# Moving the first edge layer's bias and maximum from ScalarE to VectorE in a graph layer, with longer lists of separately fetched rows

## The chip, the cores and the metric

The kernel runs on one core of a Trainium2 chip. The metric is the device time of one execution in microseconds (us); for the kernel before it is the median of three runs. The profile and the trace come from one execution under the hardware profiler. A core has five engines that work side by side and wait for each other through semaphores: TensorE (PE in the profile; PEld is its weight load), VectorE (DVE), ScalarE (ACT), GpSimd (POOL) and SyncE (SP). SPq and ACTq in a row are the queues of an engine that issue transfers.

## The reference

A graph of 6250 nodes with 128 numbers each has 106250 edges, sorted by their target node. For every edge a small network on its attributes is scaled by a gate, joined with the row of the source node, and sent through a second network; the results are added up by target node, and a residual and a normalisation follow. All is float32.

```python
ef = relu(edge_attr @ We1 + be1) @ We2 + be2
tw = sigmoid(timestamps[:, None] @ Wt + bt)
ef = ef * tw
combined = concatenate([x[row], ef], axis=1)
msg = relu(combined @ Wn1 + bn1) @ Wn2 + bn2
out = segment_sum(msg, col, num_segments=N) + x
x = layernorm(x + out)
```

## The kernel before

The kernel first multiplies x by the upper half of Wn1, adds bn1 and stores the result in HBM as `node_table`. The product with Wn2 is taken only after the sum over the edges, on whole nodes.

The edges are cut into 104 pairs of 1024 edges (two groups of four tiles of 128). A pair p is worked on over several steps; in step s, TensorE does these things in this order:

- psT: transposes of the edge attributes of pair s (L914), which ScalarE copies to `eaT`
- psS: sums of pair s - 3 by one-hot matrices (L896), after ScalarE's maximum on `h` (L656)
- psM: product of the edge features `efw` of pair s - 2 with the lower half of Wn1 (L938)
- psH: first layer of pair s (L951). Ahead of it stands a wait until the first six gathers of pair s - 2 have landed (`follow_gathers`)
- psE: second layer of pair s - 1 (L963), which reads `h1`

ScalarE makes `h1` from psH (`relu_h1`, L729: bias and maximum with 0 in one ACTIVATE) at the end of its step. VectorE does, in step s: two adds of found sums to `acc` (L1184), eight one-hots (L1226) and their count (L1234); then `pre` of pair s - 2 (L1220: psM plus the gathered rows, into `h`); then `second_layer` of pair s - 1 (L1241). Every two steps or so a block of 512 nodes is finished by all engines (`finish`).

The rows of `node_table` that `pre` adds are fetched by GpSimd with indirect transfers (L566), one for each tile of 128 edges, eight for a pair. The rows land in a ring of slots, four pairs deep (two spare pairs come in once, at pairs 8 and 9). Before the gathers of pair p, GpSimd waits until `pre` of enough pairs is done:

```python
def added_for(p):

    if p >= CLOSE_FROM:
        return p - 1
```

Below `CLOSE_FROM` the count is p - 3 (two less up to pair 13), which stands for `pre` of pair p - 4; from `CLOSE_FROM` on it stands for `pre` of pair p - 2.

For some pairs GpSimd leaves out the eighth gather. Its 128 rows are fetched one by one instead, by plain transfers that SyncE issues (pairs in `FETCHED`, 16 rows in a step, eight steps for a pair) or ScalarE issues (pairs in `ACT_FETCHED`, 8 rows in a step, 16 steps for a pair). They land in a buffer, and in step p + 1 ScalarE copies them to their place (`place_rows`). There are 11 pairs in the first list and 6 in the second. The first four pairs (0 to 3) come from x with 32 gathers of their own. So GpSimd issues 32 + 100 x 8 - 17 = 815 gathers.

All engines but GpSimd run the same order of steps, written out for the case that applies here (`most < W`).

Of the kernel before, what the change touches and what calls it, by code (L numbers as in the profile page):

```python
# [34 lines left out]
ALU = mybir.AluOpType  # L35
# [10 lines left out]
P = 128  # L46
# [30 lines left out]
PART = (6, PAIR * TILES - 6)  # L77


CLOSE_FROM = 20  # L80


SPARE = range(8, 10)


FETCH_ROWS, FETCH_STEPS = 16, 8
FETCHED = list(range(15, 96, FETCH_STEPS))


ACT_ROWS, ACT_STEPS, ACT_FROM = 8, 16, 6  # L90
ACT_FETCHED = list(range(ACT_FROM + ACT_STEPS, 103, ACT_STEPS))


def gnn_kernel(nc, x, src, dst, edge_attr, edge_weight, We1, be1, We2, be2, Wt, bt, Wn1, bn1, Wn2, bn2, out):
# [5 lines left out]
    PAIRS = G // PAIR  # L100
    BODY = 4
# [21 lines left out]
    with ExitStack() as ctx:  # L123
# [332 lines left out]
        def _(sp):  # L456
# [83 lines left out]
            for n in range(BODY, PAIRS):  # L540
                sp.wait_ge(eaT_ps, n - BODY + 1)
                load_edges(n)
                if n == BODY:
                    sp.wait_ge(src_in, 48)
                fetch_rows(n)
                sp.wait_ge(tw_ready, n - BODY + 1)
                load_weights_of(n)
            sp.wait_ge(last.y_done, 1)
            sp.dma_start(out_last, x_sb[0:LAST, FULL, 0:C]).then_inc(y_out, 16)

# [42 lines left out]
        def _(act):  # L593
# [44 lines left out]

            def fetch_rows(s):

                f, at = divmod(s - ACT_FROM, ACT_STEPS)
                if not 0 <= f < len(ACT_FETCHED) or at * ACT_ROWS >= P:
                    return
                if f == 0 and at == 0:
                    act.wait_ge(src_in, 48)
                    wait_table(act)
                if at == 0 and f > 1:
                    act.wait_ge(act_placed, f - 1)
                parts = range(at * ACT_ROWS, min((at + 1) * ACT_ROWS, P))
                rows = numbers_of(ACT_ENGINE, ACT_FETCHED[f], parts)  # L650
                for part, row in zip(parts, rows):
                    act.dma_start(act_fetched[part:part + 1, f % 2, :], table[bass.ds(row, 1), :])\  # L652
                        .then_inc(act_rows_in[f % 2], 16)
# [17 lines left out]
            def step(i, k):  # L671
                s = i * BODY + k
                if s >= PAIRS + 2:
                    if s == PAIRS + 2:
                        last_step((PAIRS - 1) % BODY * PAIR)
                    return
                if live(i, k, ADD_LAG):
                    copy_sums(s - ADD_LAG, k - ADD_LAG)
                if TILE < k <= TILE + BT // 2 and 1 <= i < TURNS:
                    finish_one(act, blocks, low["now"], lambda b: copy_tiles((k - TILE - 1) * 2), False)  # L680
                if live(i, k, H_LAG):
                    g = s - H_LAG
                    at = g % BODY * PAIR
                    act.wait_ge(pre_ready, g + 1)
                    relu(h[:, at:at + PAIR, :].rearrange("p q e -> p (q e)")).then_inc(h_ready, 1)
                if s - 1 in FETCHED + ACT_FETCHED:
                    place_rows(s - 1)
                if live(i, k, 0):
                    act.wait_ge(eaT_ps, s + 1)
                    nc.scalar.activation(eaT[:, k % 2, :], psT[:, :], ACT.Copy).then_inc(eaT_ready, 1)  # L690
                if s < RAW - RAW_BEFORE - 1:
                    copy_raw(s)
                if s == 0:
                    act.wait_ge(table_out[0], 16 * RING)
                    relu_h1(s)
                if s == 1:
                    act.wait_ge(table_out[1], 16 * RING)
                if live(i, k, 0):
                    if s < BODY:
                        for n in ([], [0], [1], [2, 3])[s]:  # L700
                            weigh(n)
                    else:
                        weigh(s)
                        fetch_rows(s)
                    if s:
                        relu_h1(s)
                if s == RAW - RAW_BEFORE - 2:
                    copy_raw(s + 1)
# [89 lines left out]
        def _(pe):  # L798
# [100 lines left out]
            def step(i, k):  # L899
# [45 lines left out]
                if live(i, k, 0):  # L945
                    follow_gathers(s, 0)
                    pe.wait_ge(eaT_ready, s + 1)
                    if raw and k == 0:
                        pe.wait_ge(src_e_ready, 2)
                    for a in range(2):  # L950
                        mm = nc.tensor.matmul(psH[:, a, :], we1[a * F:(a + 1) * F, :],  # L951
                                              eaT[a * F:(a + 1) * F, k % 2, :], start=True, stop=True)
                    mm.then_inc(h1_ps, 1)
                if raw and k in (0, 2):
                    raw_product(k)
                if live(i, k, EF_LAG):
                    if raw and k == EF_LAG:
                        pe.wait_ge(table_ready, len(JOBS))
                        pe.wait_ge(h1_ready, 1)
                    if isinstance(i, int) and s - EF_LAG == PAIRS - 1:  # L960
                        pe.wait_ge(h1_ready, PAIRS)
                    for r in range(2):
                        mm = nc.tensor.matmul(psE[:, r, :], we2[:, :], h1[:, (k - EF_LAG) % 2, r * GE:(r + 1) * GE],  # L963
                                              start=True, stop=True)
                    mm.then_inc(ef_ps, 1)
# [105 lines left out]
        def _(dve):  # L1071
# [167 lines left out]
            def second_layer(g, k):  # L1239
# [3 lines left out]
                                               tw[:, (k - EF_LAG) % 2, :], ALU.add, ALU.mult)\  # L1243
                    .then_inc(efw_ready, 1)

            def pre(g, i, k):
                place = (k - MSG_LAG) % BODY
                at = slice(place * PAIR, (place + 1) * PAIR)
                dve.wait_ge(msg_ps, g + 1)
                if isinstance(g, int) and g < RAW // PAIR:  # L1250
                    rows = raw_pairs[g]
                    if g < RAW_BEFORE // PAIR:
                        dve.wait_ge(table_ready, len(BLOCKS) + (g + 1) * PAIR)
                    else:
                        dve.wait_ge(raw_ready, (g + 1) * PAIR - RAW_BEFORE)
                else:
                    slot = (place - len(SPARE)) % BODY * PAIR
                    rows = rows_of(g) if isinstance(g, int) else gathered[:, slot:slot + PAIR, :]
                    for part in range(2):
                        landed, count = (landing(g, part) if isinstance(g, int)  # L1260
                                         else (gather_in[slot // PAIR][part], (i - 1) * (16 * PART[part])))
                        dve.wait_ge(landed, count)
                make_pre(h[:, at, :], psM[:, :, :], rows).then_inc(pre_ready, 1)

            def step(i, k):
# [38 lines left out]
                if isinstance(i, int) and s == 0:  # L1304
                    for r in range(2):
                        dve.wait_ge(dst_ps, 1 + r)
                        spread(dst_e, 1, r, dst_e_ready)
                    add_raw_bias(0)
                if live(i, k, MSG_LAG):
                    pre(s - MSG_LAG, i, k)  # L1310
                if isinstance(i, int) and s == 2:
# [262 lines left out]
```

## Time and profile before

| what | value |
|---|---|
| median of three runs (lowest, highest) | 1044.24 us (1042.26, 1045.14) |
| profiled execution: its own time, its span | 1044.55 us, 1043.1 us |
| busy share: TensorE, VectorE, ScalarE, GpSimd | 82%, 62%, 47%, 74% |
| mean granted clock of TensorE | 0.956 of full speed |

The span runs from the first to the last instruction. An engine's busy share counts the time in which an instruction ran; issuing transfers, waiting and reading registers are not counted as busy. In a row of the trace, "[0.39 <-PE psM L938]" says that the engine was idle for 0.39 us before, and that psM of TensorE ended that wait; "<-issue" means that it waited for nothing that the profile shows.

### The profile page before, as it was taken

What the parts mean: (1) busy time and instruction counts of PE and PEld (TensorE: products, weight loads), DVE (VectorE), ACT (ScalarE), POOL (GpSimd) and SP (SyncE); (2) the same over time, 40 slices, a digit from 0 to 9 for tenths busy, and PEclk for the clock granted to TensorE, in tenths of its full rate; (3) what the DMA queues carried; (4) which work ended last, traced back from release to release, by engine and by line L of the source; (5) the groups of instructions that cost most, each with busy time, mean ns of one, the idle gap of its engine ahead of it and who ended that gap; (6) DMA issues with size and microseconds to landing.
All of it is one profiled execution on the core that took longest, in us unless ns stands there. A gap on an engine that the chain in (4) does not pass through costs nothing.

```text
span 1043.1 us, 22424 instructions
## 1 busy us (share of the span) xinstructions
PE 851.1 (82%) x5035; PEld 616.5 (59%) x5036; DVE 648.9 (62%) x1682; ACT 494.9 (47%) x674; POOL 776.5 (74%) x825
## 2 busy tenths in 40 slices
PE   6989996988888778778787778878877877888884
PEld 6766665665556565555565555555555555565653
DVE  4767774775756665755557566566566566557566
ACT  5565454455445345444345445445444444444443
POOL 7777777777777777777777777777777777777772
PEclk9999999999999999999999999999999999999997
DMA  8984555555555554554545555455455455455311
GB/s 231 278 239 124 146 146 146 140 150 140 135 156 142 144 155 118 145 154 133 137 138 137 137 143 155 117 146 154 115 147 146 126 146 143 127 149 142 83 53 48
DMA packets 159417, 148.90 MB, mean 143 GB/s; under 512 B 123479, under 2 KB 127894, under 8 KB 159270
## 3 DMA queue, kind: packets, MB, share of 16 engines
q1 hardware_dynamic: 129062, 89.99, 31.0%
q0 software_dynamic: 26080, 53.46, 20.0%
q10 hardware_dynamic: 4128, 3.87, 1.2%
q8 instruction: 45, 0.74, 0.3%
q14 instruction: 102, 0.84, 0.3%
HBM read 140.85 MB, written 6.40 MB: 141 GB/s over the span
## 4 chain that ended last, share of the span: by engine, by line
POOL 44%; issue 22%; PE 12%; DMA 7%; DVE 6%; SPq 3%; ACT 3%; ACTq 1%; DVEq 1%; POOLq 0%
POOL gathered L566 44%; DMA gathered<-node_table,src_e 5%; PE psS L896 4%; PE psM L938 3%; PE psE L963 2%; DVE h L1220 2%; PE psH L951 2%; SPq L537 2%; DMA x_sb<-in_x 1%; DVE onehot L1226 1%; ACT h L656 1%; DMA ew<-in_edge_weight 1%; ACT tw L724 1%; ACTq L652 1%; DVE efw L1241 1%
## 5 line engine op out<-in xcount | busy, mean ns | idle before, releaser
L566 POOL DMA_INDIRECT gathered<-node_table,src_e x767 | 729.3, 951 | 234.0 <-issue 228.2
L729 ACT ACTIVATE h<-psH,be_c 128x1024 f32<-128x1024 f32 x104 | 115.9, 1114 | 443.1 <-PE psH L951 435.1
L896 PE MATMUL psS<-onehot,h 128*128 128x128 f32 x1656 | 226.4, 292 | 67.6 <-ACT h L656 65.7
L896 PEld LDWEIGHTS psS<-onehot,h 128*128 128x128 f32 x1656 | 209.1, 204 | 86.1 <-issue 49.4
L1220 DVE TENSOR_TENSOR h<-psM,gathered 128x1024 f32<-128x1024 f32 (+1 forms) x102 | 120.2, 1180 | 220.8 <-DMA gathered<-node_table,src_e 173.4
L963 PE MATMUL psE<-h,we 128*128 128x512 f32 x416 | 218.3, 649 | 0.0
L938 PE MATMUL psM<-wn,efw 128*128 128x128 f32 x1664 | 208.6, 280 | 4.8 <-DVE h L1220 4.8
L938 PEld LDWEIGHTS psM<-wn,efw 128*128 128x128 f32 x1664 | 200.7, 197 | 5.6 <-DVE h L1220 5.6
L1241 DVE SCALAR_TENSOR_TENSOR efw<-psE,be_c,tw 128x1024 f32<-128x1024 f32 x104 | 133.3, 1281 | 105.6 <-PE psE L963 95.5
L951 PE MATMUL psH<-eaT,we 64*128 64x512 f32 x416 | 120.1, 654 | 66.7 <-DMA gathered<-node_table,src_e 63.3
L1226 DVE TENSOR_SCALAR onehot<-split_ids,dst_e 128x65 f32<-128x65 f32 x832 | 173.9, 272 | 0.0
L963 PEld LDWEIGHTS psE<-h,we 128*128 128x128 f32 x416 | 74.3, 199 | 133.8 <-issue 133.8
L724 ACT ACTIVATE tw<-ew,bt_c,wt_c 128x1024 f32<-128x1024 f32 (+1 forms) x108 | 133.7, 1242 | 16.2 <-DVE efw L1241 15.5
L656 ACT ACTIVATE h<-h 128x1024 f32<-128x1024 f32 (+1 forms) x108 | 110.4, 1025 | 30.0 <-DVE h L1220 29.0
L1234 DVE TENSOR_REDUCE found<-onehot 128x128 f32<-128x512 f32 x104 | 108.9, 1047 | 3.6
L914 PEld LDWEIGHTS psT<-ident,ea 128*128 128x128 f32 x416 | 52.6, 143 | 56.1 <-issue 56.1
L951 PEld LDWEIGHTS psH<-eaT,we 64*128 64x128 f32 x416 | 31.7, 187 | 82.2 <-DMA gathered<-node_table,src_e 71.5
L1184 DVE TENSOR_TENSOR acc<-acc,found 128x128 f32 x204 | 58.1, 285 | 28.2 <-issue 20.2
L690 ACT ACTIVATE eaT<-psT 128x512 f32<-128x512 f32 x104 | 61.4, 590 | 9.0 <-PE psT L914 6.8
L914 PE MATMUL psT<-ident,ea 128*128 128x128 f32 x416 | 62.6, 273 | 0.0
L881 PE MATMUL psS<-wn,staged_own 128*128 128x128 f32 x88 | 20.4, 317 | 31.2 <-ACT h L656 31.2
L881 PEld LDWEIGHTS psS<-wn,staged_own 128*128 128x128 f32 x88 | 14.6, 208 | 36.0 <-issue 36.0
(128 smaller groups left out, 363.5 us busy)
## 6 DMA issues: line engine op xcount, KB each, us to landing
ew<-in_edge_weight SPq DMA_DIRECT2D x104, 512.0 KB
ea<-in_edge_attr SPq DMA_DIRECT2D x104, 256.0 KB
fetched<-node_table SPq DMA_DIRECT2D x1408, 0.5 KB
dst_rows<-node_table ACTq DMA_DIRECT2D x768, 0.5 KB
gathered<-node_table,src_e POOLq DMA_INDIRECT x767, 2.5
x_sb<-in_x SPq DMA_DIRECT2D x6, 512.0 KB, 9.0
out_y<-x_sb ACTq DMA_DIRECT2D x12, 256.0 KB
node_table<-gathered SPq DMA_DIRECT2D x7, 256.0 KB, 5.7
```

The costliest lines, as they stand in the source:

```text
L566: pool.indirect_dma_start(to, None, rows, bass.IndirectOffsetOnAxis(index, 0)).then_inc(landed, by)
L656: return nc.scalar.activation(at, at, ACT.Relu)
L724: made = nc.scalar.activation(to, of, ACT.Sigmoid, bias=bt_c[:, :], scale=wt_c[:, :])
L729: nc.scalar.activation(h1[:, s % 2, :], psH[:, :, :].rearrange("p r e -> p (r e)"), ACT.Relu, bias=be1_c[:, :]).then_inc(h1_ready, 1)
L896: return nc.tensor.matmul(to, h[:, (k - SUM_LAG) % BODY * PAIR + q, t * C:(t + 1) * C], hot, start=(t == 0), stop=(t == TILES - 1))
L914: mm = nc.tensor.transpose(psT[:, (q * 2 + a) * P:(q * 2 + a + 1) * P], ea[k // 2][:, k % 2 * PAIR + q, a * P:(a + 1) * P], ident[:, :])
L938: mm = nc.tensor.matmul(psM[:, q, t * P:(t + 1) * P], efw[:, (k - MSG_LAG) % 2, of], wn1[:, 1, :], start=True, stop=True)
L951: mm = nc.tensor.matmul(psH[:, a, :], we1[a * F:(a + 1) * F, :], eaT[a * F:(a + 1) * F, k % 2, :], start=True, stop=True)
L963: mm = nc.tensor.matmul(psE[:, r, :], we2[:, :], h1[:, (k - EF_LAG) % 2, r * GE:(r + 1) * GE], start=True, stop=True)
L1220: return nc.vector.tensor_tensor(to, of, rows, ALU.add)
L1226: made = nc.vector.tensor_scalar(onehot[:, (k - MSG_LAG) % 2, q * TILES + t, :].rearrange("p (a b) -> p a b", b=IDS), split_ids[:, :, 0:ID ...
L1241: nc.vector.scalar_tensor_tensor(efw[:, (k - EF_LAG) % 2, :], psE[:, :, :].rearrange("p r e -> p (r e)"), be2_c[:, :], tw[:, (k - EF_LAG) ...
```

## The change

From step 4 on (`BODY` is 4) the bias and the maximum of the first layer run on VectorE, as one instruction `first_layer` that reads psH and writes `h1`, in front of `pre` in each step; ScalarE keeps them for steps 0 to 3. Where the order on ScalarE used to keep buffers safe, waits are added: psH and psE on TensorE wait for `h1_ready`, ScalarE's copy to `eaT` waits for psH of two pairs before.

The lists of separately fetched rows become longer. `FETCHED` begins at 14 and goes to 102 (12 pairs). `ACT_FETCHED` has 8 pairs: 23 with 8 rows a step over 16 steps, then 33, 44, 55, 66, 77, 88 and 99 with 12 rows a step over 11 steps. `CLOSE_FROM` goes from 20 to 40.

```diff
-CLOSE_FROM = 20
+CLOSE_FROM = 40
...
-FETCHED = list(range(15, 96, FETCH_STEPS))
-
-
-ACT_ROWS, ACT_STEPS, ACT_FROM = 8, 16, 6
-ACT_FETCHED = list(range(ACT_FROM + ACT_STEPS, 103, ACT_STEPS))
+FETCHED = list(range(14, 103, FETCH_STEPS))
+
+
+ACT_FROM, ACT_PARTS = 6, [(8, 16)] + 7 * [(12, 11)]
+ACT_BEGIN = [ACT_FROM + sum(n for _, n in ACT_PARTS[:f]) for f in range(len(ACT_PARTS))]
+ACT_FETCHED = [at + n for at, (_, n) in zip(ACT_BEGIN, ACT_PARTS)]
+ACT_FETCHED = [p + (p in FETCHED) for p in ACT_FETCHED]
...
+            for n in range(PAIRS, FETCHED[-1] + 4):
+                fetch_rows(n)
...
-                f, at = divmod(s - ACT_FROM, ACT_STEPS)
-                if not 0 <= f < len(ACT_FETCHED) or at * ACT_ROWS >= P:
+                f = sum(s >= begin for begin in ACT_BEGIN) - 1
+                if f < 0:
+                    return
+                at, each = s - ACT_BEGIN[f], ACT_PARTS[f][0]
+                if at * each >= P:
                     return
...
                     act.wait_ge(eaT_ps, s + 1)
+                    if s > BODY:
+                        act.wait_ge(h1_ps, s - 1)
...
-                    if s:
+                    if 0 < s < BODY:
                         relu_h1(s)
...
                     pe.wait_ge(eaT_ready, s + 1)
+                    if not raw:
+                        pe.wait_ge(h1_ready, s)
...
-                    if isinstance(i, int) and s - EF_LAG == PAIRS - 1:
-                        pe.wait_ge(h1_ready, PAIRS)
+                    if not raw:
+                        pe.wait_ge(h1_ready, s - EF_LAG + 1)
...
+            def first_layer(g, k):
+                dve.wait_ge(h1_ps, g + 1)
+                nc.vector.tensor_scalar(h1[:, k % 2, :], psH[:, :, :].rearrange("p r e -> p (r e)"), be1_c[:, :], 0.0,
+                                        ALU.add, ALU.max).then_inc(h1_ready, 1)
...
+                if live(i, k, 0) and not (isinstance(i, int) and s < BODY):
+                    first_layer(s, k)
                 if live(i, k, MSG_LAG):
                     pre(s - MSG_LAG, i, k)
```

VectorE's row before, in step 7 (`pre` of pair 5); `found` holds sums and counts of a pair, `acc` the running totals:

```order
L1184 TENSOR_TENSOR acc<-acc,found 128x2x64
L1226 TENSOR_SCALAR onehot<-split_ids,dst_e 128x65 x4
L1234 TENSOR_REDUCE found<-onehot 128x2x64 [waits onehot_ready]
L1220 TENSOR_TENSOR h<-psM,gathered 128x1024 [waits gather_in1_1,gather_in1_0,msg_ps]
L1241 SCALAR_TENSOR_TENSOR efw<-psE,be2_c,tw 128x1024 [waits ef_ps]
```

and the same place after:

```order
L1195 TENSOR_TENSOR acc<-acc,found 128x2x64
L1237 TENSOR_SCALAR onehot<-split_ids,dst_e 128x65 x4
L1245 TENSOR_REDUCE found<-onehot 128x2x64 [waits onehot_ready]
L1259 TENSOR_SCALAR h1<-psH,be1_c 128x1024 [waits h1_ps]
L1231 TENSOR_TENSOR h<-psM,gathered 128x1024 [waits gather_in1_1,gather_in1_0,msg_ps]
L1252 SCALAR_TENSOR_TENSOR efw<-psE,be2_c,tw 128x1024 [waits ef_ps]
```

The new instruction (L1259), with its wait for psH, stands between the count of the one-hots and `pre`; all that VectorE does later in the step moves behind it.

TensorE's row before, in the same step (the matrices of one name stand in one row):

```order
L896 MATMUL psS<-onehot,h 128x128 [waits h_ready]
L896 MATMUL psS<-onehot,h 128x128 x7
L938 MATMUL psM<-wn1,efw 128x128 [waits efw_ready]
L938 MATMUL psM<-wn1,efw 128x128 x7
L951 MATMUL psH<-eaT,we1 128x512 [waits eaT_ready,gather_in1_0]
L951 MATMUL psH<-eaT,we1 128x512
L963 MATMUL psE<-h1,we2 128x512 x2
```

and after:

```order
L905 MATMUL psS<-onehot,h 128x128 [waits h_ready]
L905 MATMUL psS<-onehot,h 128x128 x7
L947 MATMUL psM<-wn1,efw 128x128 [waits efw_ready]
L947 MATMUL psM<-wn1,efw 128x128 x7
L962 MATMUL psH<-eaT,we1 128x512 [waits h1_ready,eaT_ready,gather_in1_0]
L962 MATMUL psH<-eaT,we1 128x512
L974 MATMUL psE<-h1,we2 128x512 [waits h1_ready]
L974 MATMUL psE<-h1,we2 128x512
```

Nothing moves on TensorE; psH and psE get a wait for `h1_ready`, which VectorE now raises.

## Rows read from the trace of the kernel before

**Rows 1.** The chain of work that ended last: shares of the span by engine.
```profile
POOL 44%; issue 22%; PE 12%; DMA 7%; DVE 6%; SPq 3%; ACT 3%; ACTq 1%; DVEq 1%; POOLq 0%
```

**Rows 2.** Waits of GpSimd before gathers: us in total, times, longest us.
```profile
POOL gathered L566 <- issue: 228.2, 748, 0.4
...
POOL gathered L566 <- DVE h L1220: 5.8, 19, 0.3
```

**Rows 3.** Groups of instructions by shape: busy us, mean ns, idle before, releaser.
```profile
L566 POOL DMA_INDIRECT gathered<-node_table,src_e x767 | 729.3, 951 | 234.0 <-issue 228.2 <-DVE h L1220 5.8
...
L1241 DVE SCALAR_TENSOR_TENSOR efw<-psE,be_c,tw 128x1024 f32<-128x1024 f32 x104 | 133.3, 1281 | 105.6 <-PE psE L963 95.5 <-issue 5.7 <-ACT tw L724 4.1
...
L1220 DVE TENSOR_TENSOR h<-psM,gathered 128x1024 f32<-128x1024 f32 x97 | 118.6, 1223 | 220.8 <-DMA gathered<-node_table,src_e 173.4 <-PE psM L938 47.3
```

**Rows 4.** Timeline (start, duration in us): GpSimd's first and last of 815 gathers.
```profile
3.27 1.10 POOL L566 DMA_INDIRECT h<-in_x,raw_e  x1 [1.31 <-DMA raw_e<-in_src]
...
1025.97 0.96 POOL L566 DMA_INDIRECT gathered<-node_table,src_e  x1 [0.30 <-issue]
```

**Rows 5.** Timeline of a middle step, 52.
```profile
503.49 3.18 ACTq L652 DMA_DIRECT2D dst_rows<-node_table  x8
503.60 6.82 SPq L537 DMA_DIRECT2D fetched<-node_table  x16
...
506.49 0.94 POOL L566 DMA_INDIRECT gathered<-node_table,src_e  x1 [0.30 <-issue]
...
507.62 1.13 PE L951 MATMUL psH<-eaT,we 64*128 64x512 f32 x4 [1.43 <-DMA gathered<-node_table,src_e]
...
508.79 1.11 ACT L729 ACTIVATE h<-psH,be_c 128x1024 f32<-128x1024 f32 x1 [4.88 <-PE psH L951]
...
510.16 1.22 DVE L1220 TENSOR_TENSOR h<-psM,gathered 128x1024 f32<-128x1024 f32 x1 [4.66 <-DMA gathered<-node_table,src_e]
...
510.25 0.95 POOL L566 DMA_INDIRECT gathered<-node_table,src_e  x1 [0.31 <-issue]
```

**Rows 6.** Timeline: first layers of pairs 4, 12; `pre` of 10; pair 14's first gather.
```profile
68.83 1.11 ACT L729 ACTIVATE h<-psH,be_c 128x1024 f32<-128x1024 f32 x1 [3.33 <-PE psH L951]
...
128.56 1.22 DVE L1220 TENSOR_TENSOR h<-psM,gathered 128x1024 f32<-128x1024 f32 x1 [0.37 <-PE psM L938]
...
129.63 1.11 ACT L729 ACTIVATE h<-psH,be_c 128x1024 f32<-128x1024 f32 x1 [3.11 <-PE psH L951]
...
144.09 0.94 POOL L566 DMA_INDIRECT gathered<-node_table,src_e  x1 [0.31 <-issue]
```

**Rows 7.** Timeline: `pre` of pair 39 and the first gather of pair 41.
```profile
404.08 1.22 DVE L1220 TENSOR_TENSOR h<-psM,gathered 128x1024 f32<-128x1024 f32 x1 [1.31 <-PE psM L938]
...
408.60 0.94 POOL L566 DMA_INDIRECT gathered<-node_table,src_e  x1 [0.30 <-issue]
```

**Rows 8.** Timeline of an early step, 11: maximum, psS, psM, psH.
```profile
115.94 1.06 ACT L656 ACTIVATE h<-h 128x1024 f32<-128x1024 f32 x1
...
117.06 2.05 PE L896 MATMUL psS<-onehot,h 128*128 128x128 f32 x16
...
118.95 1.95 PE L938 MATMUL psM<-wn,efw 128*128 128x128 f32 x16
...
120.82 1.13 PE L951 MATMUL psH<-eaT,we 64*128 64x512 f32 x4
```

**Rows 9.** Timeline near the end: `pre` of pair 101.
```profile
1009.35 1.23 DVE L1220 TENSOR_TENSOR h<-psM,gathered 128x1024 f32<-128x1024 f32 x1 [4.24 <-DMA gathered<-node_table,src_e]
```

**Rows 10.** Timeline: an add of VectorE at a gather's start.
```profile
149.06 0.28 DVE L1184 TENSOR_TENSOR acc<-acc,found 128x128 f32 x1
...
149.10 1.06 POOL L566 DMA_INDIRECT gathered<-node_table,src_e  x1 [0.30 <-issue]
```

**Rows 11.** Stretches: each engine's busy us, TensorE's granted clock, transfer share, GB/s.
```profile
100.00:150.00 50.00, 47.41 (x294) 33.99 (x293) 35.85 (x89) 27.67 (x35) 37.94 (x40) 1.00 0.53 135
...
200.00:250.00 50.00, 42.04 (x235) 30.34 (x232) 32.35 (x86) 24.96 (x34) 37.89 (x40) 0.93 0.54 140
```

More of the change, by code:

```diff
@@ L648, in fetch_rows @@
                     act.wait_ge(act_placed, f - 1)
-                parts = range(at * ACT_ROWS, min((at + 1) * ACT_ROWS, P))
+                parts = range(at * each, min((at + 1) * each, P))
                 rows = numbers_of(ACT_ENGINE, ACT_FETCHED[f], parts)
```

## The prediction, made before the changed kernel ran

> **What bounds the kernel now.** I read the chain that ended last first. It spends 44% of the span on GpSimd's gathers (L566) and 22% on "issue" [rows 1]. Then I asked what GpSimd waits for. Of its idle time before the gathers from the table, 228.2 us are 748 pauses of at most 0.4 us in which it waited for nothing that the profile shows; only 19 waits name VectorE, and the longest of those is 0.3 us, the same pause [rows 2]. So GpSimd never really stands still. One gather takes 951 ns [rows 3], and with a pause of 0.30 us consecutive starts lie 1.25 us apart. The first gather starts at 3.27 us and the last of 815 at 1025.97 us [rows 4]: a mean distance of (1025.97 - 3.27) / 814 = 1.256 us, which is almost the bare 1.25. The time is therefore the number of gathers times 1.256 us, a start of 3 us, and a tail of 1043.1 - 1026.0 = 17.1 us.
>
> The other engines show the same from their side. In a middle step the last gather of pair 50 starts at 506.49, psH of pair 52 starts at 507.62, released when the first six gathers of pair 50 have landed, and `pre` of pair 50 starts at 510.16, released when all have landed [rows 5]. Compute waits for gathers there.
>
> This was not so early on. GpSimd starts gathering pair 14 at 144.09 (its 113th gather: 32 + 10 x 8 lie before it), and by then `pre` has only got to pair 10 at 128.56 and a little further: compute is catching up, at (129.63 - 68.83) / 8 = 7.60 us a step, with 10 us of gathers for a pair [rows 6]. There only the rule on slots could hold GpSimd.
>
> **The change, part by part.**
>
> *Fewer gathers.* SyncE's list grows from 11 to 12 pairs, ScalarE's from 6 to 8: 20 skipped gathers instead of 17, so 812 instead of 815, and 3 x 1.256 = 3.8 us less. All three come off before pair 101: up to there 19 are skipped now and 16 before; of pair 102 one is skipped either way.
>
> *The first layer on VectorE.* 100 instructions of 128x1024 with one operand, from PSUM. The trace has none. Nearest are VectorE's add with one of two operands from PSUM, 1223 ns, and its two-step second layer, 1281 ns [rows 3]; ScalarE's version takes 1.11 us [rows 5]. I take 1.22 us, the row it is nearest to, with 1.11 and 1.28 as ends. What hides it is the landing. It can start when psH ends, 507.62 + 1.13 = 508.75, and ends about 508.80 + 1.22 = 510.02; `pre` started at 510.16 [rows 5]. It fits with 0.14 us to spare (0.08 at 1.28, 0.25 at 1.11). In a pair with seven gathers the last landing is 1.25 us earlier, and `pre` slips by 1.1 us. Queued behind the new wait for psH are `pre`, the second layer and the next step's adds and one-hots; for `pre` wait ScalarE's maximum, TensorE's sums and, by the rule on slots, GpSimd. From pair 40 on (before: from 20) GpSimd may start pair p when `pre` of p - 2 is done. A tight case is 408.60 for pair 41 against 404.08 + 1.22 for pair 39, a gap of 3.3 us [rows 7]. A slip of 1.1 us is covered three times over and costs nothing; with that cover gone, 20 slips of 1.1 us would be 22 us.
>
> *ScalarE* loses 100 x 1.11 us and issues 1024 row transfers instead of 768, twelve in a step instead of eight from step 22 on. Eight take 3.18 us, so twelve take 4.8: 503.49 + 4.8 = 508.3, earlier than the 508.79 up to which it used to wait for psH, and than `pre` at 510.16, which its next maximum needs [rows 5]. Hidden. *SyncE* issues 16 rows in 6.82 us [rows 5] of a step of 10 us, as before; the new ones lie one step earlier at the front and in the last eight steps. Hidden. *TensorE's* new waits on `h1_ready`, before psH and psE, both ask for a first layer that VectorE ran a step earlier: no price.
>
> *The catch-up.* Here the first layer is on the path, since nothing waits for gathers. One loop is then psH 1.13 [rows 5], first layer 1.22, `pre` 1.22 [rows 3], ScalarE's maximum 1.06, psS to psM 118.95 - 117.06 = 1.89, psM to psH 120.82 - 118.95 = 1.87 [rows 8], and four hand-overs of some 0.05: 8.6 us, 1.0 more than 7.60. The first of these steps is 4 and `pre` of pair 10 runs in step 12, so it starts at 128.56 + 8 x 1.0 + 2.3 (psH and the first layer now lie ahead of it in its own step) = 138.9 and ends at 140.1. GpSimd wants it at 144.09, to start pair 14: the rule for pairs under 40 asks for `pre` of p - 4. That leaves 4.0 us. Pair 15 comes 8.75 us later and needs pair 11, 8.6 us later; from there GpSimd takes 10 us a pair and compute 8.6, and the gap grows. No price. The higher bound, 40 for 20, takes away a rule that could bite while compute is still behind.
>
> *The tail.* `pre` of pair 101 starts at 1009.35, released by its gathers [rows 9], and what follows hangs on it. The first layer of pair 103 lies in front of it as at 508.80. Bounds are 0 and 0.3 us; I take 0.1.
>
> **The sum.** The profiled run took 1044.55 us, 0.3 over the median of 1044.24. 1044.55 - 3.8 + 0.1 = 1040.85; less the 0.3, **1040.6 us** as a median, 0.35% below. The three runs before spread over 2.9 us, so 0.3% (3.1 us) is about what a measurement here can tell from no change, and the forecast lies just beyond it.
>
> **A rule that speaks against it.** Some gathers take longer. The one at 149.10 took 1.06 us instead of 0.94, and a VectorE add of two SBUF tensors had started at 149.06 [rows 10]. The gather at 510.25, beside `pre` with one operand from PSUM, took 0.95 [rows 5]. The Trainium skill, "GPSIMD Engine Reference", section "Key points", says that GpSimd shares its SBUF interfaces with VectorE, in contention with instructions that have two SBUF inputs or run in a 2-port mode. The trace agrees, at 0.12 us a hit. By that rule the new instruction, which reads a tensor from PSUM alone, costs the gathers nothing itself; but it can shift the adds against the gathers' starts, which is the first rival.
>
> **The rivals.**
> 1. *The adds move onto the gathers.* There are 204 adds of `acc`, two a step, at 0.12 us a hit. All gathers together now lie 814 x (1.256 - 1.25) = 5 us over the bare distance, so some 40 hits at most. The adds follow `pre` at a fixed distance; if the first layer delays `pre` by a tenth or two in most steps, 25 more hits make 3 us: 1043.6, no change. If 20 hits fall away: 1038.2. For it: 0.14 us to spare is thin. Against it: a hit needs the add near a gather's start, and `pre` follows the landings, in the gathers' own grid.
> 2. *GpSimd waits at pair 14* (the other side). From a loop of 8.6 + 4.0 / 8 = 9.1 us on, GpSimd is stopped there, by 8 us for each further us of loop. Slower by 0.3% needs a stop of 3.8 + 3.1 = 6.9 us, a loop of 9.97: 1047.5 and more. TensorE would now wait about 1 us in one piece in each loop and could be granted less clock: its 4.9 us of the loop double at the lower level, 1.2 GHz, and 28% of that work there, a mean clock of 0.78, would do. Against it: the granted clock was 1.00 from 100 to 150 us, and even with the longer waits of 200 to 250 us it was 0.93 [rows 11], which adds 0.4 us to a loop.
> 3. *The end does not follow.* VectorE works almost without a pause behind `pre` of 101; if the first layers of the last two steps both lie on that path, less the time under the landing, the tail grows by 1.2 to 2.4 us: 1042.4, no change. Against it: ScalarE did the same layer in nearly the same time under the landing.
>
> **How the numbers follow.** Forecast 0.60 (own range 1039.2 to 1042.0); fewer hits 0.10; more hits 0.13; the end does not follow 0.07; GpSimd waits at pair 14, 0.10. The forecast lies only 0.5 us from 1041.1, the bound of 0.3%, so 0.43 of its 0.60 count as faster; with the 0.10 of fewer hits, 0.53. Slower are most of rival 2 and a little of rival 1: 0.11. The rest, 0.36, is the same. The range goes from fewer hits, 1038.2, to a stop of 4.4 us at pair 14, 1045.0; beyond lie about 0.08 above and 0.06 below.
>
> **What would show it.** Right: 812 gathers at a mean distance of 1.25 to 1.26 us; no wait of GpSimd over 0.5 us at pairs 10 to 20 or at 40; the new instruction at 1.11 to 1.28 us, and `pre` at the landing or just behind it; steps of 8.3 to 8.9 us from 70 to 150 us; the last gather at about 1022.2 us and a tail still of 17 us. Wrong: a wait for VectorE in front of a gather, gathers of more than 0.955 us in the mean, a tail over 18 us.

## The result and the profile after

The changed kernel takes 1053.19 us (median of five runs, 1049.34 to 1056.71), the kernel before 1044.24 us (five runs, 1041.83 to 1045.14). The ratio is 1.0101, with a 95% interval of [1.0069, 1.0132]: about 1% slower, where 0.35% faster was forecast. The profiled run of the changed kernel took 1049.34 us, of which the span is 1047.5; it is the fastest of the five.

The chain that ended last, shares of the span by engine in the changed kernel, against [rows 1]:

```profile
PE 30%; issue 20%; POOL 17%; DVE 14%; ACT 7%; ACTq 6%; DMA 5%; DVEq 1%; SPq 1%; POOLq 0%
```

GpSimd's part fell from 44% to 17%; TensorE, VectorE and ScalarE together now hold 51%. Up to GpSimd's first long wait, at 402.91 us, the chain holds no gather at all and runs round the loop of the three compute engines; 175 us of gathers lie on it behind that wait.

The waits of the changed kernel (us in total, times, longest us), answering to [rows 2, 3]:

```profile
POOL gathered L570 <- issue: 226.5, 742, 0.3
DVE h L1259 <- PE psH L962: 226.3, 91, 7.0
ACT h L663 <- DVE h L1231: 187.1, 85, 8.0
PE psS L905 <- ACT h L663: 123.6, 79, 3.4
...
PE psH L962 <- DMA gathered<-node_table,src_e: 21.2, 19, 2.5
POOL gathered L570 <- DVE h L1231: 16.9, 22, 5.8
```

VectorE waits for psH 91 times, ScalarE's maximum for `pre`, TensorE's sums for the maximum: each waits for the next, round in a circle. TensorE still waits for gathers in 19 steps, before psH. And GpSimd, whose longest wait for VectorE was 0.3 us, now has one of 5.8 us.

The groups by shape of the changed kernel (busy us, mean ns, idle before, releaser), against [rows 3]:

```profile
L570 POOL DMA_INDIRECT gathered<-node_table,src_e x764 | 725.5, 950 | 243.4 <-issue 226.5 <-DVE h L1231 16.9
...
L1259 DVE TENSOR_SCALAR h<-psH,be_c 128x1024 f32<-128x1024 f32 x100 | 128.2, 1282 | 226.6 <-PE psH L962 226.3 <-issue 0.3
...
L1231 DVE TENSOR_TENSOR h<-psM,gathered 128x1024 f32<-128x1024 f32 x97 | 117.8, 1214 | 0.4 <-DMA gathered<-node_table,src_e 0.3
```

The last row is the shortest statement of what happened. `pre` used to wait 173.4 us for gathers; now it waits 0.3 us. Its rows had always landed when VectorE came to it, so the first layer ahead of it was hardly ever hidden under a landing.

**Where GpSimd stands.** The timeline of GpSimd's gathers after (start, duration), at pairs 14, 40 and 41 and the last of the 812, against [rows 4, 6, 7]:

```profile
143.98 0.94 POOL L570 DMA_INDIRECT gathered<-node_table,src_e  x1 [0.30 <-issue]
...
402.91 0.94 POOL L570 DMA_INDIRECT gathered<-node_table,src_e  x1 [5.81 <-DVE h L1231]
...
417.71 0.94 POOL L570 DMA_INDIRECT gathered<-node_table,src_e  x1 [4.96 <-DVE h L1231]
...
1031.33 0.94 POOL L570 DMA_INDIRECT gathered<-node_table,src_e  x1 [0.30 <-issue]
```

At pair 14 nothing stops it. At pairs 40 and 41, the first ones under the tighter rule, it stands for 5.81 and 4.96 us, 10.2 us more than two usual pauses. The last gather starts at 1031.33, not at the 1022.2 that was forecast, although the mean gather is as long as before (950 ns). The rest of the span, 16.2 us, is the tail.

**The loop early on.** The timeline of the changed kernel from psH of step 8 to psH of step 9, one turn of the loop:

```profile
102.79 1.13 PE L962 MATMUL psH<-eaT,we 64*128 64x512 f32 x4
...
103.97 1.28 DVE L1259 TENSOR_SCALAR h<-psH,be_c 128x1024 f32<-128x1024 f32 x1 [1.91 <-PE psH L962]
...
105.17 1.21 DVE L1231 TENSOR_TENSOR h<-psM,gathered 128x1024 f32<-128x1024 f32 x1
...
106.41 1.06 ACT L663 ACTIVATE h<-h 128x1024 f32<-128x1024 f32 x1 [1.36 <-DVE h L1231]
...
107.94 2.05 PE L905 MATMUL psS<-onehot,h 128*128 128x128 f32 x16 [1.68 <-ACT h L663]
...
109.83 1.95 PE L947 MATMUL psM<-wn,efw 128*128 128x128 f32 x16
...
111.71 1.13 PE L962 MATMUL psH<-eaT,we 64*128 64x512 f32 x4
...
112.89 1.28 DVE L1259 TENSOR_SCALAR h<-psH,be_c 128x1024 f32<-128x1024 f32 x1 [1.54 <-PE psH L962]
```

The first layer starts when psH ends, `pre` when the first layer ends, and so on round to the next psH. From one first layer to the next this turn takes 8.92 us; `pre` of pairs 4 to 14 lie 8.67 us apart in the mean (7.52 before). That is the forecast loop of 8.6.

**The loop later.** The distance of each `pre` from the one before, for pairs 15 to 38, worked out from their starts in the timeline (us; eight steps, in which a block is finished, to a line):

```
10.08  9.66  8.51  8.50  10.34  10.26  8.51  8.50
13.48  9.66  8.51  8.50  10.42  10.56  8.51  8.50
10.13  9.67  8.50  8.50  10.82   8.92  8.51  8.50
```

A bare step, one without work on a block, takes 8.50 us. But a block of 512 nodes falls due in every eighth step (6250 / 512 = 12.2 blocks in 104 steps; the "two steps or so" in the description of the kernel before is wrong), and its finishing lengthens four of the eight. The mean is 226.05 / 24 = 9.42 us, and GpSimd needs 187 gathers x 1.256 / 24 = 9.79 us for a pair here, because some pairs have seven gathers. The next step, to pair 39, is one of 14.80 us; the mean for pairs 16 to 39 is 9.62 us, so the figure of 9.42 leaves the longest step out. Measured from the end of GpSimd's last gather of a pair to the start of its `pre`, compute lags 22.1 us behind at pair 16 and still 13.9 us at pair 38 (before: 12.3 at 16, and 3.2 by 36). Then comes the rule that asks for `pre` of p - 2: pair 40 waits for the `pre` of pair 38, and pair 41 for that of 39, between which lies a long step. It is shown by the timeline of step 40 of the changed kernel:

```profile
400.92 1.22 DVE L1231 TENSOR_TENSOR h<-psM,gathered 128x1024 f32<-128x1024 f32 x1
...
402.00 2.12 ACT L766 ACTIVATE staged_own<-acc 128x512 f32 x2 [5.67 <-issue]
...
404.19 1.04 ACT L663 ACTIVATE h<-h 128x1024 f32<-128x1024 f32 x1
...
405.81 0.77 PE L890 MATMUL psS<-wn,staged_own 128*128 128x128 f32 x2 [3.79 <-ACT h L663]
...
407.65 3.62 PE L905 MATMUL psS<-onehot,h 128*128 128x128 f32 x16
...
415.72 1.22 DVE L1231 TENSOR_TENSOR h<-psM,gathered 128x1024 f32<-128x1024 f32 x1
```

and by its stretches (columns as in [rows 11]):

```profile
100.00:150.00 50.00, 42.49 (x258) 29.78 (x256) 37.30 (x79) 15.59 (x22) 37.96 (x40) 1.00 0.55 147
200.00:250.00 50.00, 41.46 (x239) 28.97 (x238) 38.83 (x94) 16.79 (x26) 37.79 (x41) 0.97 0.56 147
400.00:420.00 20.00, 14.58 (x73) 11.36 (x72) 11.84 (x27) 8.12 (x11) 9.59 (x10) 0.83 0.38 111
```

`pre` ends at 402.14, but ScalarE is copying a finished block until 404.12, so its maximum starts 2.05 us after the end of `pre` (0.03 in the early turn). TensorE has stood for 3.79 us, multiplies the block's tiles first, and psS takes 3.62 us instead of 2.05, in a stretch with a granted clock of 0.83. The next `pre` comes 14.80 us after this one.

**Run to run.** Times of the changed kernel against TensorE's mean granted clock: 1049.34 at 0.974, 1052.66 at 0.965, 1053.19 at 0.964, 1056.53 at 0.960, 1056.71 at 0.958. The time rises as the clock falls; which of the two follows from the other was not tested. The kernel before shows nothing of that (1043.07 at 0.942, 1044.60 at 0.959), and between versions it is the other way round: experiments 2 and 3 were profiled at 0.954, a lower clock than the 0.974 of the profiled run of the changed kernel, and are faster. The four runs that were not profiled were 3 to 7 us slower than the profiled one.

### The profile page after: what moved, and what is told of

It is laid out like the page before. It is cut to its first block, busy times and chain, and to the rows that moved or that the text cites. A ratio compares the mean times of both kernels' runs of the same rounds, so it can differ in the third digit from the quotient of the medians.

```text
span 1047.5 us, 23685 instructions
## 1 busy us (share of the span) xinstructions
PE 832.8 (80%) x5035; PEld 608.8 (58%) x5036; DVE 760.4 (73%) x1782; ACT 389.6 (37%) x577; POOL 772.5 (74%) x822
## 4 chain that ended last, share of the span: by engine, by line
PE 30%; issue 20%; POOL 17%; DVE 14%; ACT 7%; ACTq 6%; DMA 5%; DVEq 1%; SPq 1%; POOLq 0%
POOL gathered L570 17%; PE psS L905 11%; PE psM L947 9%; DVE h L1231 8%; PE psH L962 6%; ACT h L663 5%; ACTq L659 4%; DMA gathered<-node_table,src_e 4%; DVE onehot L1237 1%; PE psS L890 1%; ACTq L412 1%; DMA x_sb<-in_x 1%; DVE h L1259 1%; PE psS L891 1%; ACTq L384 1%
## 5 line engine op out<-in xcount | busy, mean ns | idle before, releaser
L1259 DVE TENSOR_SCALAR h<-psH,be_c 128x1024 f32<-128x1024 f32 x100 | 128.2, 1282 | 226.6 <-PE psH L962 226.3
L974 PE MATMUL psE<-h,we 128*128 128x512 f32 x416 | 206.1, 618 | 0.0
L628 ACT ACTIVATE found<-psS 128x128 f32<-128x128 f32 x103 | 28.4, 276 | 330.5 <-issue 301.1
L974 PEld LDWEIGHTS psE<-h,we 128*128 128x128 f32 x416 | 70.5, 189 | 127.1 <-issue 127.1
L962 PE MATMUL psH<-eaT,we 64*128 64x512 f32 x416 | 117.4, 641 | 21.2 <-DMA gathered<-node_table,src_e 21.2
```

The source lines that it names most:

```text
L1259: nc.vector.tensor_scalar(h1[:, k % 2, :], psH[:, :, :].rearrange("p r e -> p (r e)"), be1_c[:, :], 0.0, ALU.add, ALU.max).then_inc(h1_rea ...
```

## The experiments

Each kernel was compared with runs of the kernel before on the same chip: 1044.60 us (13 runs) for the first four, 1045.29 (16 runs) for the next four, 1044.56 (17 runs) for the last. Theory A: the close rule from pair 40 costs the time. Theory B: compute itself, with the layer in front of `pre`, is no faster than the gathers. Theory C: the longer lists cost it.

**1. The rule never closes.** The edit in the changed kernel:

```diff
-CLOSE_FROM = 40
+CLOSE_FROM = 104
```

> The changed kernel with CLOSE_FROM at 104, so that GpSimd may always run ahead until pre of p - 4. Theory A (the stop at pair 40 is the loss: compute is still 13.9 us behind the gathers at pair 38, the tighter rule stops GpSimd for 5.8 and 5.0 us): no wait of GpSimd for VectorE over 0.5 us; steps from 16 to 40 took 9.42 us in the mean against 9.75 us of gathers, so compute gains 0.33 us a step and the 14 us are made up by about pair 82; the last gather at 1022 us, time 1040 to 1042 us. Theory B (with the first layer on VectorE compute needs as long for a step as GpSimd for a pair, and the rule only shows it): the lag stays above 8 us to the end, tail 25 us and more, time 1047 to 1054 us. Theory C (twelve rows a step on ScalarE hold up the maximum): as B, with the long steps of 13 to 15 us where ScalarE stages a block.

Measured: 1048.72 us (1041.87 to 1053.05, ten runs), ratio 1.003 [1.0006, 1.0055]; the profiled run took 1050.18. The timeline of this kernel, `pre` of pair 101, the last gather, and `pre` of pair 102:

```profile
1016.01 1.21 DVE L1231 TENSOR_TENSOR h<-psM,gathered 128x1024 f32<-128x1024 f32 x1
...
1020.14 0.94 POOL L570 DMA_INDIRECT gathered<-node_table,src_e  x1 [0.30 <-issue]
...
1027.43 1.21 DVE L1231 TENSOR_TENSOR h<-psM,gathered 128x1024 f32<-128x1024 f32 x1
```

GpSimd never waits for more than 0.6 us and ends 11.2 us earlier than in the changed kernel. But the run ends at 1048.4: the tail is 28.2 us instead of 16.2. From pair 14 on `pre` stays 14 to 27 us behind the gathers all the way (23.3 at pair 40, 14.1 at 101), and neither psH nor `pre` waits for a gather, so compute goes here at its own pace: 9.60 us a step in the mean from pair 40 to 101, which gains 0.15 us a pair on the gathers. The time lies where theory B expected it, not where A did (1040 to 1042), and most of the delay is there without the stop. Some of it is not: the median is 4.5 us below that of the changed kernel, and the intervals of the two ratios do not overlap. Against experiment 3, the best version, the changed kernel loses 14.3 us and this one 9.8, so by the medians A accounts for about a third. How firm that share is stays open: the two profiled runs, 1049.34 and 1050.18, do not show it. A way in which a stop can cost is that the gathers then come only just ahead of compute, and TensorE waits for them in 19 steps of the changed kernel; this was not tested apart.

**2. The first layer behind `pre`.** The edit in VectorE's step:

```diff
-                if live(i, k, 0) and not (isinstance(i, int) and s < BODY):
-                    first_layer(s, k)
                 if live(i, k, MSG_LAG):
                     pre(s - MSG_LAG, i, k)
+                if live(i, k, 0) and not (isinstance(i, int) and s < BODY):
+                    first_layer(s, k)
```

> The changed kernel with the first layer behind pre instead of in front of it, all else the same. Theories A and B (the layer stands in the loop psH, first layer, pre, maximum, psS, psM, psH): the loop loses the first layer and psH's wait, early steps of 7.5 to 7.9 us instead of 8.5 to 8.9, compute has caught up before pair 40, no stop of GpSimd, time 1040 to 1041.5 us. Theory C: the maximum is still held up by the rows and the staging, steps of 13 us where a block is staged, time 1045 to 1050 us.

Measured: 1039.62 us (1039.12 to 1040.37, four runs), ratio 0.9951 [0.9934, 0.9967]. The waits of this kernel:

```profile
POOL gathered L570 <- issue: 227.9, 747, 0.3
...
DVE h L1231 <- DMA gathered<-node_table,src_e: 146.2, 60, 5.1
```

`pre` waits for landings again, and GpSimd for nothing over 0.3 us. Early steps take 7.91 us, the lag of `pre` behind the gathers is 1.6 us at pair 20, and the last gather starts at 1020.87. The time is 0.4 us under the range expected. The same instructions, in another order, bring the gain that was forecast for the change.

**3. The first layer stays on ScalarE, lists and rule as changed.** The core of the edit:

```diff
-                    if 0 < s < BODY:
+                    if s:
                         relu_h1(s)
...
-                if live(i, k, 0) and not (isinstance(i, int) and s < BODY):
-                    first_layer(s, k)
```

(the added waits for it go too).

> The changed kernel's lists and CLOSE_FROM of 40, but the first layer stays on ScalarE as before. Theories A and B: early steps of 7.6 us until step 22, caught up by pair 30, no stop, the three gathers come off: 1040 to 1042 us. Theory C: ScalarE has the layer behind twelve rows, which end 1.6 us later than eight did, so the steps from 22 on grow by 1 us and more, and compute is late in the steps in which ScalarE stages a block: 1044 to 1050 us.

Measured: 1038.91 us (1038.59 to 1039.64, four runs), ratio 0.9944 [0.9928, 0.9961], the fastest version of all. This is 1.1 us under the range expected; the early steps (pairs 4 to 14) took 8.05 us in the mean and not 7.6, because one of 12.7 us is among them, in which ScalarE waits 4.7 us for fetched rows. The lag is 6.6 us at pair 20, there is no stop, the last gather starts at 1020.08. The longer lists and the rule from 40 do no harm by themselves; twelve rows a step fit on ScalarE beside the first layer.

**4. The first layer in front of `pre`, lists as before.** The core of the edit:

```diff
-FETCHED = list(range(14, 103, FETCH_STEPS))
+FETCHED = list(range(15, 96, FETCH_STEPS))
...
-ACT_FROM, ACT_PARTS = 6, [(8, 16)] + 7 * [(12, 11)]
+ACT_FROM, ACT_PARTS = 6, 6 * [(8, 16)]
```

> The first layer on VectorE in front of pre, with CLOSE_FROM of 40, but the lists of before (17 pairs, eight rows a step on ScalarE). Theory A: early steps of 8.5 to 8.9 us, GpSimd is stopped at pair 40 and 41 by some 5 to 12 us in all, with 815 gathers: 1049 to 1056 us. Theory B: the same, 1050 to 1056 us. Theory C (the rows do it): steps without the 13 to 15 us, compute caught up by pair 40, no stop, 1044 to 1045 us.

Measured: 1049.90, 1051.63 and 1056.94 us; a fourth run, of 2785.62 us, more than twice the others, is left out. The ratio is 1.009 [1.0055, 1.0125]. The profiled run has the stop at pair 40 again, of 9.3 us, with only eight rows a step on ScalarE. Theory C falls: the lists do not make the delay. The run also tells the blocks' work from the rows that SyncE fetches, which come round every eight steps too: in these lists the fetched pairs lie one later, and yet the long steps end at the same pairs as in the changed kernel (11.71 us to pair 15, 12.07 to 23, 10.18 to 31, 10.47 to 39).

**5. More work in front of `pre`.** A second reading of psH by VectorE, ahead of the first layer (the line that allots its result is left out here):

```diff
                 dve.wait_ge(h1_ps, g + 1)
+                wait(dve, twice_done, g - BODY)
+                nc.vector.tensor_reduce(twice[:, :], psH[:, :, :].rearrange("p r e -> p (r e)"), AX_X, ALU.max)\
+                    .then_inc(twice_done, 1)
```

> The changed kernel with one more VectorE instruction of 1024 columns in front of the first layer (a maximum over psH, some 1.2 us, its result unused). Theory B (all steps run at the pace of the loop through the first layer): steps of 10.9 us instead of 9.7, 100 times 1.2 us more, time 1160 to 1175 us, GpSimd stopped in front of most pairs. Theory A (only the stop at pair 40 costs, in the middle the landing hides VectorE): the early steps are longer, the stop at pair 40 is longer by 30 to 40 us, later steps stay near 9.8: 1080 to 1095 us.

Measured: 1176.96 us (1176.23 and 1177.69), ratio 1.1257 [1.1232, 1.1282]. The groups of this kernel:

```profile
L571 POOL DMA_INDIRECT gathered<-node_table,src_e x764 | 725.5, 950 | 364.6 <-issue 215.1 <-DVE h L1232 149.5
...
L1261 DVE TENSOR_REDUCE twice<-psH 128x1 f32<-128x1024 f32 x100 | 122.4, 1224 | 252.0 <-PE psH L963 251.9
```

A hundred instructions of 1.22 us, 122.4 us of work, cost 1176.96 - 1053.19 = 124 us over the changed kernel. No part of it is hidden. GpSimd now waits 149.5 us for VectorE, and from pair 40 to 101 a step takes 10.85 us, against the 10.9 that theory B expected; the time is 2 us over its range and far from that of theory A.

**6. Half of the layer in front of `pre`.** The edit:

```diff
-                nc.vector.tensor_scalar(h1[:, k % 2, :], psH[:, :, :].rearrange("p r e -> p (r e)"), be1_c[:, :], 0.0,
+                nc.vector.tensor_scalar(h1[:, k % 2, 0:GE], psH[:, 0, :], be1_c[:, :], 0.0,
```

> The changed kernel with only half of the first layer's columns computed (the other half of h1 is left as it was, so half of that work is left out): 0.55 us less in front of pre. Theory B: early steps of 8.1 instead of 8.67 us, steps with the blocks' work 8.9 us in the mean, faster than GpSimd's 9.75, so compute catches up near pair 40 and GpSimd is stopped for 0 to 4 us: 1039 to 1044 us, and the runs lie within 3 us of each other. Rival (not the length but the added hand-over and the new waits cost): 1047 us and more.

Measured: 1040.77 us (1037.89 to 1042.77, seven runs), ratio 0.9963 [0.995, 0.9976]. Early steps of 8.14 us, a lag of 4.6 us at pair 40, and only two short stops of GpSimd (1.05 and 1.35 us). The time is as theory B expected, though its steps with blocks came out longer (9.31 us in the mean for pairs 15 to 38, not 8.9) and the runs lie 4.9 us apart, not 3. The instruction takes 750 ns instead of 1282; 0.5 us less in a step is enough to bring the kernel back to the gathers.

**7. Behind `pre`, with the lists of before.** Edits 2 and 4 together.

> The first layer on VectorE behind pre, with the lists of before (815 gathers). If the move as such is worth nothing once it is out of the loop: 1042.5 to 1044.5 us, the time of before. Rival (a freed ScalarE gains by itself): 1041 us or less, with shorter steps where a block is staged.

Measured: 1045.01 us (1044.16 to 1046.63, ten runs), ratio 0.9996 [0.9986, 1.0006], 0.5 us over the range expected and the time of the kernel before. With 815 gathers the moved layer is worth nothing, although ScalarE has 100 x 1.11 us less to do. The gain of experiments 2 and 3 comes with the longer lists, the three gathers less.

**8. One gather less, by thirteen rows a step on ScalarE.** Edit 2, and:

```diff
-ACT_FROM, ACT_PARTS = 6, [(8, 16)] + 7 * [(12, 11)]
+ACT_FROM, ACT_PARTS = 5, [(8, 16)] + 8 * [(13, 10)]
```

> The first layer behind pre, and a ninth pair for ScalarE (thirteen rows a step over ten steps), 811 gathers. If gathers alone set the time: 1.25 us under the 1039.6 of the run with 812, 1038.0 to 1038.8 us. Rival (ScalarE, at 5.1 us of rows a step, becomes late for its maximum): over 1041 us, with GpSimd stopped in places.

Measured: 1103.51 us (1102.13 to 1105.29, four runs), ratio 1.055 [1.0531, 1.0568]: the expectation was missed by far. The chain of this kernel, by engine and by line:

```profile
PE 40%; ACTq 27%; issue 11%; ACT 11%; DVE 7%; SPq 2%; DMA 1%; DVEq 0%
ACTq L659 17%; PE psS L905 13%; PE psM L947 9%; PE psE L974 9%; ACTq L412 7%; ACT tw L733 5%; PE psH L962 5%; DVE efw L1252 5%; ACT h L663 4%; ACTq L384 2%; SPq L539 1%; PE psS L890 1%; DMA x_sb<-in_x 1%; PE psS L891 1%; PE psT L923 0%
```

ScalarE's issuing (L659), with the loading of the row numbers (L412), has come onto the chain. Steps of pairs 15 to 38 take 10.15 us, the later ones 10.5; the lag grows from 5.4 us at pair 20 to 20.8 at 36, and GpSimd stands 10.46 us at pair 40. In a step near 500 us, thirteen rows take ScalarE 5.17 us here, against 4.72 for twelve in experiment 2:

```profile
499.73 5.17 ACTq L659 DMA_DIRECT2D dst_rows<-node_table  x13
```
```profile
502.40 4.72 ACTq L659 DMA_DIRECT2D dst_rows<-node_table  x12
```

That is half a us more in a step, and the steps grew by 0.7 us over experiment 2 (9.48 us for pairs 15 to 38). That ScalarE is the bound is read from this trace; it was not tested apart.

**9. Smaller copies of finished blocks.** This tests the cause named above, the blocks' share of the loop, in the changed kernel itself; ScalarE copies one column in 128 and leaves out the rest:

```diff
+            for to in (staged_counts, staged_sums):
+                nc.scalar.activation(to, zero_c[:, :].to_broadcast([P, BT * C]), ACT.Copy)
...
-                    nc.scalar.activation(to.rearrange("c (t p) -> c t p", t=BT),
-                                         of[:, bass.ds(b * BN, BN)].rearrange("c (p t) -> c t p", t=BT), ACT.Copy)\
+                    nc.scalar.activation(to.rearrange("c (t p) -> c t p", t=BT)[:, :, 0:1],
+                                         of[:, bass.ds(b * BN, BN)].rearrange("c (p t) -> c t p", t=BT)[:, :, 0:1],
+                                         ACT.Copy)\
```

(The first two lines clear the buffers once, before the loop.)

> As the changed kernel, but ScalarE's two copies of a finished block (128x512 each, 2.12 us together, eleven times) copy one column in 128; the work left out is the rest of these copies, so that the sums of most nodes are never finished. Everything else, the waits too, stays. Theory B (compute is as slow as the gathers because the blocks' work lengthens half of its steps: 8.50 us without a block, 9.7 to 14.8 us with one): the step behind a copy falls by about 2 us, and the long steps of 13 and 15 us, in which TensorE had also lost clock, mostly go. Two us in eight steps take the mean step of pairs 15 to 38 from 9.42 to about 9.1 us; GpSimd needs 9.79 us a pair, so compute gains 24 x 0.3 = 7 us more on the gathers by pair 38, the stops of GpSimd at pairs 40 and 41 fall from 10.2 us to under 4, and the median lies at 1040 to 1047 us. Rival (the loop with the layer in front of pre is slow by itself, by hand-overs or by clock, and the blocks only sit beside it): mean step 9.4 and stops of 8 us or more as before, 1050 to 1056 us.

Measured: 1041.28 us (1038.02 to 1047.88, twelve runs), ratio 0.9971 [0.9952, 0.9991]. The groups of this kernel, and the timeline of GpSimd at pairs 40 and 41:

```profile
L768 ACT ACTIVATE staged_own<-acc 128x4 f32 x22 | 3.4, 204 | 52.4 <-issue 52.4
```
```profile
399.26 0.94 POOL L570 DMA_INDIRECT gathered<-node_table,src_e  x1 [2.82 <-DVE h L1234]
...
410.97 0.94 POOL L570 DMA_INDIRECT gathered<-node_table,src_e  x1 [1.93 <-DVE h L1234]
```

Early steps are as before this edit (8.67 us), those of pairs 15 to 38 take 9.25 instead of 9.42 (9.1 was expected), and the stops fall from 10.2 us over the usual pauses to 2.82 + 1.93 - 0.60 = 4.2. Eleven times 2.12 us on ScalarE, less the 3.4 us that remain, is 20 us of work; taking it out lowers the median by 11.9 us, more than the change had lost (9.0). The copies of the blocks are indeed on the path of the changed kernel. They are not all of the blocks' share: half of the steps still take 8.94 to 11.70 us.

## Why the prediction was wrong

**Fewer gathers: right.** 812 instead of 815. Experiment 3 against the kernel before gives 5.7 us, experiment 2 gives 5.0. Three gathers at 1.256 are 3.8 of these; the rest is the mean distance, 1.2538 and 1.2547 us instead of 1.2564, times 812: 2.1 and 1.4.

**The first layer: right in size, wrong in place.** 1282 ns, at the upper bound, the row of the second layer. The step "What hides it is the landing" was read from step 52 of before [rows 5], where compute waited for gathers. In the changed kernel `pre` almost never does (0.3 us in all), and psH, ahead of the layer, for 21.2 us, so the layer's 128 us stand in compute's own loop and not under a landing.

**The catch-up: its loop right to 0.1 us, as far as it went.** A loop of 8.67 where 8.6 was forecast; `pre` of pair 10 at 140.01 instead of 138.9; a slack of 143.98 - 141.23 = 2.75 us at pair 14 instead of 4.0, and no stop there.

**The step that failed: "from there GpSimd takes 10 us a pair and compute 8.6, and the gap grows. No price."** Neither figure holds from step 16 on. GpSimd takes 9.79, because of the pairs with seven gathers, and compute 9.42, because finishing a block lengthens four of eight steps. The gap closes by 0.37 us a pair (by 0.17 if the long step to pair 39 is counted), not 1.4, and 24 pairs of it are 9 us of the 22 by which compute lagged; at 1.4 they would have been 34. So at pair 38 it was still 13.9 us behind. The rows behind the 8.6 [rows 8] come from a step without a block. The kernel before had the same blocks, but early steps 1.15 us shorter. Experiment 6 takes 0.5 us off each step, experiment 9 some 2 us of ScalarE's work off each eighth one, and either brings the time back to 1041 us.

**The close rule: wrong side.** "A slip of 1.1 us is covered three times over" supposed that compute had caught up; and the higher bound, said to take away a rule that could bite, put it at a pair where it bit. This is the mechanism of the second rival, GpSimd stopped by `pre`, at pair 40 instead of 14 and without the clock that the rival called for (1.00 from 100 to 150 us, 0.97 from 200 to 250). Yet experiment 1 shows that the stop is not the root: without it about two thirds of the loss, by the medians, is paid at the end.

**The sum, term by term**, for the profiled run: forecast 1040.85, measured 1049.34, 8.5 us more. The stops of 10.2 us and 1.1 us saved on the other distances move the last gather by 9.1; the tail is 1.0 shorter than the 17.2 forecast; the time outside the span is 1.84 instead of 1.45, 0.4 more. The median lies another 3.9 us higher, with a lower clock in the runs that were not profiled; there is no trace of these.

**The gathers' contention: right.** The Trainium skill, "GPSIMD Engine Reference", section "Key points", names contention with GpSimd for VectorE's instructions with two SBUF inputs or in a 2-port mode; the new instruction reads one tensor, from PSUM. The trace agrees: 950 ns a gather with it, 951 without.

**What stays open.** How the 9.6 to 9.7 us of the steps after pair 40 divide into blocks, clock and other waits was not taken apart; nor was thirteen against twelve rows a step, nor the way in which the stop costs more in the median than the longer tail that takes its place.

## What to carry to other kernels

Whether a piece of work is hidden is a property of a stage, so price a loop over a whole period of everything that runs in it, here eight steps with a block, before calling one engine faster than another. Where two rates lie within a few per cent of each other, as here, a us in front of the instruction that the loop hangs on can cost in full (experiment 5), and the same us behind it can be free (experiments 2 and 7). A stop of the old bottleneck engine may only show a delay that is made elsewhere: take the stop away and see whether the time comes back.

## What the runs showed of the hardware that was not expected

- Kernels paced by the gathers repeat within 0.1 to 0.6% (experiments 2, 3 and 7 and the kernel before), the changed kernel and experiments 1 and 9, where compute and gathers are nearly as fast as each other, within 0.7 to 1.1%, and their longer runs show a lower granted clock of TensorE (in experiment 1, 1041.87 us at 0.962 and 1053.05 at 0.952). That the clock is the cause was not tested. That compute sets the pace is not enough for such a spread: experiments 5 and 8, where it is slower than the gathers by far, repeat within 0.1 and 0.3% (two and four runs).
- The same 16 matrices of psS took 2.05 us in the bare step and 3.62 after TensorE had stood for 3.79 us, in a stretch with a granted clock of 0.83; there one long wait in the loop was followed by a second delay.
- Plain transfers of one row cost the engine that issues them about 0.4 us each (twelve 4.72 us, thirteen 5.17), and one more in a step, for one gather less, turned 1039.62 us into 1103.51.
